# Attention layers: VectorE adds the residual between the first subtraction and the division, and takes the statistics behind the division

## The reference

```python
# layer 1 ("L1_xattn"): 16 heads, keys from the context
x = x + attention(layernorm(x), ctx)
# layer 2 ("L2_xattn"): 16 heads, keys from the context, mask * -1e9 added to the scores
x = x + attention(layernorm(x), ctx, mask)
# layer 2, second half ("L2_ffn"): 8 heads, keys from x itself (128), own norm, cut widths
x = x + self_attention(layernorm(x))
# with
scores = q @ k.T * scale            # per head
p = exp(scores - max(scores))
out = (p @ v) / sum(p)              # the division by head sums comes last
out = out @ Wo + bo
```

## Time and profile before

| | |
|---|---|
| median of three runs | 4488.58 us (4487.06 to 4490.65) |
| the profiled execution | 4493.48 us |
| its span | 4491.7 us |
| PE busy | 3291.8 us, 73% |
| DVE busy | 3271.1 us, 73% |
| ACT busy | 2302.0 us, 51% |
| POOL busy | 1518.8 us, 34% |
| layer 1, residuals first to last | 1143.3 to 1515.3 us |
| the self layer's row maxima (L684), first to last | 2542.0 to 2889.7 us |

### The profile page before, as it was taken

One profiled execution on the slowest core, in us unless ns is written; L12 is line 12 of the kernel. 1 busy time (PEld: TensorE's weight loads), 2 busy tenths in 40 slices (PEclk: granted clock), 3 DMA queues, 4 the chain that ended last, 5 costly groups with the idle time before them and its releaser, 6 DMA issues. The chain is left out here.

```text
span 4491.7 us, 84327 instructions
## 1 busy us (share of the span) xinstructions
PE 3291.8 (73%) x23624; PEld 1988.5 (44%) x23624; DVE 3271.1 (73%) x12675; ACT 2302.0 (51%) x4265; POOL 1518.8 (34%) x1262
## 2 busy tenths in 40 slices
PE   4777778998999699998999688766776666311168
PEld 1222224443677444444667455444554444211055
DVE  6999985665788565565888577699999999533254
ACT  5999993333566344443666455555555555100020
POOL 5777761000100122223444422221122112566550
PEclk9999999999999899998999899855555556555575
DMA  2000005000000000000000000000000000200026
GB/s 66 4 4 4 4 4 225 0 0 5 7 7 6 23 0 1 0 0 8 13 13 13 7 0 0 7 4 3 4 4 3 3 4 3 95 21 1 8 86 191
DMA packets 110380, 95.86 MB, mean 21 GB/s; under 512 B 64780, under 2 KB 95704, under 8 KB 107005
## 3 DMA queue, kind: packets, MB, share of 16 engines
q1 hardware_dynamic: 86654, 78.97, 6.1%
q0 software_dynamic: 14336, 10.87, 0.8%
q10 hardware_dynamic: 9216, 4.20, 0.3%
HBM read 55.57 MB, written 57.97 MB: 25 GB/s over the span
## 5 line engine op out<-in xcount | busy, mean ns | idle before, releaser
L394 PE MATMUL PS<-IDENT,a_T 128*77 128x128 f32 (+1 forms) x3584 | 616.5, 311 | 130.3 <-ACT a_Pr L524 109.1
L986 ACT ACTIVATE l_H<-l_H 128x2048 f32<-128x2048 f32 (+2 forms) x256 | 598.2, 2727 | 2.9 <-POOL l_H L1038 2.7
L394 PEld LDWEIGHTS PS<-IDENT,a_T 128*77 128x77 f32 (+1 forms) x3584 | 485.8, 171 | 224.1 <-ACT a_Pr L524 114.8
L1038 POOL TENSOR_TENSOR l_H<-l_feat,l_text 128x4096 f32<-128x4096 f32 x64 | 450.5, 7040 | 131.1 <-PE PS L942 130.5
L942 PE MATMUL PS<-l_H,l_wide 128*32 128x512 f32 (+1 forms) x2560 | 331.7, 594 | 163.2 <-ACT l_H L986 163.2
L1060 DVE TENSOR_TENSOR l_H<-PS,l_text 128x2048 f32<-128x2048 f32 (+1 forms) x192 | 411.9, 2147 | 2.1 <-ACT l_text L1013 2.1
L526 ACT ACTIVATE a_Pr<-PS 77x512 f32<-77x512 f32 (+1 forms) x640 | 375.4, 587 | 55.4 <-PE PS L394 53.1
L608 POOL TENSOR_TENSOR a_T<-a_mx,a_T 128x616 f32<-128x616 f32 x128 | 155.6, 1216 | 726.9 <-DVE a_mx L666 726.9
L409 PE MATMUL PS<-a_Pr,a_vaug 77*32 77x128 f32 (+1 forms) x7168 | 307.1, 318 | 12.5 <-issue 8.3
L1980 POOL DMA_INDIRECT expert_rows<-e3r_row,e3r_rows_at x256 | 253.0, 988 | 138.2 <-issue 89.8
L339 PE MATMUL PS<-a_kblk,a_qT 32*128 32x308 f32 (+1 forms) x2048 | 242.2, 548 | 12.5 <-ACT a_kblk L538 5.4
(11 more groups left out here) (292 smaller groups left out, 8299.2 us busy)
## 6 DMA issues: line engine op xcount, KB each, us to landing
expert_shares<-e_zero SPq DMA_DIRECT2D x16, 1024.0 KB, 22.0
e3c_four<-expert_shares SPq DMA_DIRECT2D x64, 256.0 KB, 3.2
e3x_xin<-expert_rows SPq DMA_DIRECT2D x32, 200.0 KB
expert_rows<-e_zero SPq DMA_DIRECT2D x6, 1024.0 KB, 8.7
a_cT<-in_ctxT SPq DMA_DIRECT2D x128, 38.5 KB, 1.7
X<-in_x SPq DMA_DIRECT2D x8, 512.0 KB, 7.2
e_w<-in_L_ffn_w SPq DMA_DIRECT2D x1, 4096.0 KB, 13.5
expert_rows<-e3r_row,e3r_rows_at POOLq DMA_INDIRECT x256
```

The lines of the kernel that those rows point to most:

```text
L394: last = pe.transpose(PS[0:keys, 4 + g % 2, j * S:(j + 1) * S], T[:, u, c:c + keys], m.IDENT[:, :])
L986: act.activation(cells, cells, ACT.Tanh).then_inc(q[f"tanh{part}"], 1)
L1038: pool.tensor_tensor(H[:, a, lo * S:hi * S].rearrange("p (t f) -> p t f", f=S), bcast(feat[:, a, :], 1, hi - lo), bcast(text[:, a, lo:hi], ...
```

## The change

In the step of VectorE, for all attention layers but the lowrank one, the residual goes behind the first `subtract_max`, and the statistics go behind the division. No instruction is added or dropped, and no other engine's code is touched.

```diff
@@ -783,13 +783,14 @@
                     if real(s - 1):
                         replace_rest(s - 1, a)
                     return
+                if real(s):
+                    subtract_max(s, u, h, 0)
                 if real(fin):
                     residual(fin, (v - lag - 2) % 2)
-                    statistics(fin)
-                if real(s):
-                    subtract_max(s, u, h, 0)
                 if real(end):
                     norm_heads(end, (v - lag - 1) % 2)
+                if real(fin):
+                    statistics(fin)
                 if real(s):
                     subtract_max(s, u, h, 1)
                 if real(s + 1):
```

## The result

The changed kernel takes 4650.24 us (median of 4 runs, 4645.11 to 4653.36) against 4488.63 us before; the ratio is 1.0359, 95% interval 1.0341 to 1.0377. It is slower by 161.6 us; 148.8 were forecast (4637 us, range 4598 to 4672). The profiled execution took 4653.36 us with a span of 4651.6, 159.9 longer than before. Runs were taken on different chips, and the kernel before measured 4417 to 4489 us beside them, so experiments are compared by their ratio to the runs of before on the same chip.

What follows compares the result with a forecast made beforehand. No engine is full; a ring of waits between DVE and PE sets the slot. Stalls of 51.0 and 59.4 us plus 38.4 us for the statistics, 148.8 in all, gave 4637 us, range 4598 to 4672.

Steps and rivals of the forecast that it cites:

- The ring and the lost cover: Slot length: waits through k, project_out, scores, L418, division, second subtraction, v; both moved instructions leave idle time that hid them.
- The size of the stall: L365 waiting for the moved residual (L753): 0.85 us a slot in layer 1, 0.99 in the mask layer, 0 in self.
- the gain of the earlier maxima: First maxima on DVE start earlier once residual and statistics no longer precede them: 0.03 us a slot.
- The statistics: Behind the division, between product and second half on DVE: 0.21 us in each of 183 slots, 38.4 us.
- The registers of L753: Register setting for the residual in its new place, beside the running instruction: 0, at most 13.2 us.
- hidden statistics: Rival: PE as late as DVE at L432 and L435, so the statistics cost nothing; 4599 us, chance 12%.
- an absorbed stall: Rival: L365 waits for an older sequence and stays in place, only the statistics cost; 4527 us, chance 3%.
- no slowing: Rival: x is up before PE reaches L365 and PE hides the statistics; 4483 us, chance 2%.
- a falling clock: Rival: TensorE's clock drops in layer 1 and the mask layer because PE idles more; 4964 us, chance 6%.

Runs made afterwards that it cites:

- e8: Kernel before, with the residual moved behind the first subtraction and the statistics at the slot's start, one sequence later; ratio 1.0278.
- e5: Changed kernel, with the residual one instruction earlier, ahead of the subtraction (behind the maxima, or the mask instructions in the mask layer); ratio 1.0135.
- e3: Changed kernel, with PE's context projection (L365, L366) behind the transposes for the division and the last two groups of transposes of T; ratio 1.0082.
- e2: Kernel before, with only the statistics moved behind the division and the residual left first in the slot; ratio 1.0068.
- e6: Kernel before, with v and k (L744, L735) ahead of the second half's subtraction in the two layers with a context; 4450.88 us, ratio 0.9925.
- e4: Kernel before, with PE's context projection (L365, L366) behind the transposes for the division and the last two groups of transposes of T; ratio 1.0049.

## Why the prediction was right, and where its sizes were off

*The ring and the lost cover*: right. L365 waits for L753 in the two layers and not in the third; e8 keeps that wait and drops the other term, e5 shortens the wait, e3 is without it, and each time the time follows.

*The size of the stall*: mis-sized, low. The sum had 0.85 and 0.99 us a slot; e8 measured 1.02 and 1.15. The residual came when forecast: L753 starts 1307.07 - 1306.35 = 0.72 us after L686, as L744 did. What was short is the step from it to the reciprocal. I took 0.09 us from the end of the residual to L365, it is 1307.49 - 1307.35 = 0.14; and I moved L418 with L365 rigidly, 0.40 us behind it, where after a stall it is 1307.97 - 1307.49 = 0.48. That makes 0.13 a slot of the missing 0.17 and 0.16. The other 0.03 is the gain of the earlier maxima, which both of my figures held and which did not come: L684 starts 1305.51 - 1304.16 = 1.35 us after the end of k, and before the change, with residual and statistics in front of it, it was 1305.89 - 1304.54 = 1.35 too. Over 60 slots in two layers the term was 130 us and not 110.

*The statistics*: 0.20 us in the layers with 16 heads as forecast (0.21), 0.15 to 0.17 in the self layer; why a part of it is hidden there was not followed up. 183 slots: 34 us, not 38. The distance from start to start, which the Trainium skill's exception (VectorE: DVE Perf Modes, "The DRAIN you can't avoid") allows, is what was paid, not the full 0.28.

*The registers of L753*: cost nothing in the new place, as taken; the 0.72 above shows it.

*What is left between the terms and the spans*: 130 + 34 = 164 us, the spans have 159.9. The first scores (L339) of layer 1 and of layer 3, before the change and after it, stand at:

```profile
1124.48 1.41 PE L339 MATMUL PS<-a_kblk,a_qT 32*128 32x308 f32 x8 [0.49 <-ACT a_qT L532]
...
2915.05 1.41 PE L339 MATMUL PS<-a_kblk,a_qT 32*128 32x308 f32 x8 [1.78 <-ACT a_kblk L538]
```

```profile
1127.39 1.41 PE L339 MATMUL PS<-a_kblk,a_qT 32*128 32x308 f32 x8 [0.49 <-ACT a_qT L532]
...
3081.53 1.41 PE L339 MATMUL PS<-a_kblk,a_qT 32*128 32x308 f32 x8 [1.78 <-ACT a_kblk L538]
```

So the changed layers took 1790.57 us and take 1954.14, which is 163.6 more, as the terms say. The other layers, whose code is the same, took 3.7 us less in all in this execution: 2.9 more ahead of layer 1 and 6.6 less from layer 3 on. I didn't look into that; single executions of one kernel lay up to 8 us apart here. It is luck that this and the overrated statistics made up for some of the underrated stall: the forecast missed the three layers by 14.8 us, the spans by 11.1.

*The rivals*: hidden statistics (e2 shows them in full in the layers with 16 heads), an absorbed stall, no slowing, and a falling clock (1.00 in all windows) did not come.

## What to carry to other kernels

Before moving an instruction into another engine's idle time, look up who waits for what it releases. Here 0.29 us of work put into a gap of 0.24 us cost 1.0 us, since the instruction that waits for it (L365) stood in PE's queue ahead of one that the ring needs (L418). L365 had 1.42 us to spare; the move spent all of it and made L365 0.92 us late. The gap in front of the scores had hidden residual and statistics at no cost that shows, and the way to gain was to shorten the ring (e6), not to fill its gaps.

## What the runs showed of the hardware

A matmul that has to wait for another engine is dearer than the same one in a running queue. L365 stands at 0.42 us after the stall and at 0.34 us before, and what follows it starts 0.08 us later; in e5, where PE shows no idle time before it but it still starts 0.15 us after the residual's end, it is 0.42 us too. Its weight load shows a difference. Before the change it starts 0.11 us ahead of its matmul (1306.95), in the changed kernel only 0.03 us ahead (1307.49):

```profile
1306.84 0.30 PEld L365 LDWEIGHTS PS<-a_cT,a_Wk 128*128 128x128 f32 x2
```

```profile
1307.46 0.30 PEld L365 LDWEIGHTS PS<-a_cT,a_Wk 128*128 128x128 f32 x2 [0.96 <-issue]
```

The query projection (L378), which the change doesn't touch, shows the same. Before the change it starts 0.15 us after the end of ScalarE's L526 (1308.20 + 0.59 us), for which it waits by the code, and takes 0.46 us; in e4 it comes right behind L424 and takes 0.39:

```profile
1308.20 0.59 ACT L526 ACTIVATE a_Pr<-PS 77x512 f32<-77x512 f32 x1 [0.19 <-PE PS L394]
...
1308.91 0.30 PEld L378 LDWEIGHTS PS<-a_yT,a_Wq 128*128 128x128 f32 x2 [0.31 <-issue]
1308.94 0.46 PE L378 MATMUL PS<-a_yT,a_Wq 128*128 128x128 f32 x2
```

```profile
1305.67 0.30 PEld L378 LDWEIGHTS PS<-a_yT,a_Wq 128*128 128x128 f32 x2
1305.78 0.39 PE L378 MATMUL PS<-a_yT,a_Wq 128*128 128x128 f32 x2
```

In both lines the longer time goes with a weight load that starts 0.03 instead of 0.11 us ahead. Whether that is the cause was not tried.
